# Stage of the maxima in a graph-attention layer: its window loop written out, with five product blocks in front and two and one by turns, and two groups of node values between the halves of a projection

## The reference

```python
xr = jnp.einsum('nd,rdf->rnf', x, W)
oi = xr[etype, dst]
oj = xr[etype, src]
qi = oi @ q
kj = oj @ k
alpha = jax.nn.leaky_relu(qi + kj, NEG_SLOPE)
m = jax.ops.segment_max(alpha, dst, num_segments=n_nodes)
e = jnp.exp(alpha - m[dst])
```

## Time and profile before

| | |
|---|---|
| median of 3 runs | 1886.23 us (1881.67 to 1899.82) |
| the profiled execution, its time | 1884.94 us |
| its span | 1883.2 us |
| TensorE matmul busy | 1677.3 us (89%) |
| VectorE busy | 1332.5 us (71%) |
| ScalarE busy | 775.4 us (41%) |
| GpSimd busy | 250.7 us (13%) |
| mean granted TensorE clock | 0.938 |

### The profile page before, as it was taken

One profiled execution on the slowest core, in us unless ns is written; L12 is line 12 of the kernel. 1 busy time (PEld: TensorE's weight loads), 2 busy tenths in 40 slices (PEclk: granted clock), 3 DMA queues, 4 the chain that ended last, 5 costly groups with the idle time before them and its releaser, 6 DMA issues.

```text
span 1883.2 us, 36980 instructions
## 1 busy us (share of the span) xinstructions
PE 1677.3 (89%) x10771; PEld 1230.7 (65%) x10772; DVE 1332.5 (71%) x2635; ACT 775.4 (41%) x1020; POOL 250.7 (13%) x268
## 2 busy tenths in 40 slices
PE   2799999999999999579999999877998889999976
PEld 1465677778755556369999999874554555555534
DVE  6777877758515899948888787861376267777776
ACT  2232112222105555258787777762121133333342
POOL 2200000000000111000000000001001023333334
PEclk9899999989998999789999999986999999999988
DMA  4111114233354343261004031123456350011112
GB/s 159 61 46 50 53 56 115 75 93 107 126 200 164 110 139 103 89 190 55 28 28 139 28 111 55 44 69 106 125 179 210 112 201 18 32 50 50 61 59 82
DMA packets 122819, 177.59 MB, mean 94 GB/s; under 512 B 12604, under 2 KB 96452, under 8 KB 122232
## 3 DMA queue, kind: packets, MB, share of 16 engines
q1 hardware_dynamic: 122744, 176.61, 29.0%
HBM read 118.75 MB, written 57.84 MB: 94 GB/s over the span
## 4 chain that ended last, share of the span: by engine, by line
PE 69%; DVE 12%; issue 9%; DMA 5%; ACT 2%; DVEq 2%; POOL 1%; SPq 1%; ACTq 0%; POOLq 0%
PE ps L1889 20%; PE ps L1947 7%; PE ps L1946 7%; PE ps L1670 6%; PE ps L1671 6%; PE ps L1672 6%; PE ps L1688 5%; PE ps L1752 3%; PE ps L1731 3%; DVE tt_junk L1417 2%; DMA xr_d<-ev 1%; PE ps L1809 1%; DVE oh_q L1282 1%; PE ps L1980 1%; DVE oh_p L1284 1%
## 5 line engine op out<-in xcount | busy, mean ns | idle before, releaser
L1889 PE MATMUL ps<-xrh,pf 128*128 (+1 forms) x2400 | 407.4, 334 | 30.9 <-DVE pf L1501 24.9
L1889 PEld LDWEIGHTS ps<-xrh,pf 128*128 128x128 f32 x2400 | 403.7, 195 | 34.7 <-issue 33.8
L1670 PE MATMUL ps<-w_hi,xt_hi 128*128 128x384 f16 x960 | 320.8, 334 | 31.2 <-DVE ev L1532 19.9
L1671 PE MATMUL ps<-w_lo,xt_hi 128*128 128x384 f16 x960 | 320.9, 334 | 0.0
L1672 PE MATMUL ps<-w_hi,xt_lo 128*128 128x384 f16 x960 | 320.4, 334 | 0.0
L1282 DVE TENSOR_SCALAR oh_q<-pat,codeT,neg_w 125x630 f16<-125x630 uint16 x420 | 200.0, 476 | 52.7 <-PE ps L1688 43.3
L1501 DVE SCALAR_TENSOR_TENSOR pf<-vb,CT 128x1260 f32<-128x1260 f32 x120 | 175.6, 1468 | 55.5 <-PE ps L1889 55.5
L1946 PE MATMUL ps<-x,ph 128*128 (+1 forms) x600 | 196.4, 327 | 19.4 <-POOL pl L871 19.4
L1947 PE MATMUL ps<-x,ph 128*128 (+1 forms) x600 | 197.9, 330 | 0.0
L1497 DVE SCALAR_TENSOR_TENSOR vb<-vb,tb 128x1260 f32<-128x1260 f32 x120 | 174.5, 1468 | 31.7 <-ACT vb L1064 30.6
L1417 DVE CUSTOM_DVE_ANT_0 tt_junk<-kbc,mb 126x1260 bf16<-126x1260 f32 x120 | 185.4, 1582 | 1.3
(11 more groups left out here) (226 smaller groups left out, 2323.1 us busy)
## 6 DMA issues: line engine op xcount, KB each, us to landing
qbc<-tq_d SPq DMA_DIRECT2D x12, 1260.0 KB, 5.8
wst<-in_L_gnn_W SPq DMA_DIRECT2D x12, 1152.0 KB, 7.4
xr_d<-ev SPq DMA_DIRECT2D x60, 192.0 KB, 2.0
xrh<-xr_d SPq DMA_DIRECT2D x4, 2880.0 KB, 15.9
x_d<-ev SPq DMA_DIRECT2D x60, 192.0 KB, 2.3
x<-x_d SPq DMA_DIRECT2D x3, 3840.0 KB, 13.6
mb_d<-mb SPq DMA_DIRECT2D x30, 310.1 KB
mb<-mb_d SPq DMA_DIRECT2D x30, 310.1 KB
```

The lines of the kernel that those rows point to most:

```text
L1670: pe.matmul(ps[:, bank, 0:CW], a_hi, hi[:, k, :], start=(k == 0), stop=False)
L1671: pe.matmul(ps[:, bank, 0:CW], a_hi, lo[:, k, :], start=False, stop=False)
L1889: mm = pe.matmul(out[b], pf[j][:, b * DB:b * DB + P], x, start=(first and b % 2 == 0), stop=False, skip_group_check=True)
```

## The change

The window loop is no longer a hardware loop on any engine but written out, and its order is new. Five blocks (`N0`) run ahead of window 0's; `products_of(w)` gives two blocks to even windows and one to odd ones, so that the 50 blocks of the loop are spread over all 30 windows. TensorE transposes the mask of window w + 2 (was w + 1) behind the blocks of window w. `maxima` writes straight to `mkt`, with four junk tiles in place of two, and waits for results further back. The node values of heads 3 and 2 are computed between the halves of the output projection. The high part of a weight chunk is made behind the last block of the chunk before it, and SyncE loads the next chunk behind the fifth store of each chunk. Cut to its core:

```diff
+        def products_of(w):
+            return range(N0 + (3 * w + 1) // 2, N0 + (3 * w + 4) // 2)
...
 # SyncE
-            loaded = 4
-            for m in range(2, loaded):
-                weights_load(sp, m)
...
+            weights_load(sp, 2)
+            def store_product(n):
+                sp.wait_ge(g_free, 6 * NB + n + 3)
+                store_xr(sp, n // NB, n % NB, n % 2)
+                if n in (N0 - 1, NB + N0 - 1, 2 * NB + N0 - 1):
+                    weights_load(sp, n // NB + 3)
+            store_mask(0)
+            for n in range(N0):
+                store_product(n)
+            for w in range(NW):
+                if w >= 1:
+                    store_mask(w)
+                for n in products_of(w):
+                    store_product(n)
...
 # ScalarE
-            w_hi_part(C_X + 1)
...
+            act.wait_ge(g_done, 6 * NB)
+            node_values(0)
+            node_values(1)
+            act.wait_ge(acc_out, 16 * 2 * NB)
             act.wait_ge(ct_in[0], 16 * 4)
...
+            def product_out(n):
+                xr_part(n, n // 2, n % 2)
+                if n % NB == NB - 1 and n // NB + 2 < 2 * R:
+                    w_hi_part(C_X + n // NB + 2)
+            def mask(w):
+                if w >= 2:
+                    act.wait_ge(mt_tr, w - 1)
...
+            def mask_out(w):
+                o = 1024 * (4 - 2 * (w % 2))
+                act.wait_ge(mt_tr, w + 1)
+                if w >= 2:
+                    act.wait_ge(mk_step, H * (w - 1))
+                    act.wait_ge(mb_out[w % 2], 16 * (w // 2))
...
+            mask(0)
+            node_values(2)
+            node_values(3)
+            mask_out(0)
+            mask(1)
+            w_hi_part(C_X + 1)
+            for n in range(N0):
+                product_out(n)
+            for w in range(NW):
+                if w >= 1:
+                    mask_out(w)
+                    if w == 20:
+                        act.wait_ge(ct_in[1], 16)
+                    if w + 1 < NW:
+                        mask(w + 1)
+                for n in products_of(w):
+                    product_out(n)
...
 # VectorE
+            for w in range(NW):
+                dve.wait_ge(mb_done, w + 1)
+                for h in range(H):
+                    q = H * w + h
+                    if h % 2 == 0:
+                        if w >= 1:
+                            dve.wait_ge(mk_step, q - 2)
+                        dve.memset(tick[:, h // 2:h // 2 + 1], 0.0)
+                    dve.tensor_tensor_reduce(out=tt_junk[h][0:WK, :], in0=kbc[0:WK, h, :], in1=mb[w % 2][0:WK, :], scale=1.0, scalar=2 * BIG,
+                                             op0=ALU.subtract, op1=ALU.max, accum_out=mkt[0:WK, h, w:w + 1]).then_inc(mk_step, 1)
...
 # TensorE
+                if c == 0:
+                    pe.wait_ge(kc_free, 1)
+                    pe.wait_ge(kr_out, NRG)
+                    pe.wait_ge(sel_done, 2)
+                    node_values(0)
+                    node_values(1)
...
+            def mask_rows(w):
                 pe.wait_ge(mt_done, w + 1)
+                if w >= 2:
+                    pe.wait_ge(mb_done, w - 1)
...
+            for n in range(2):
+                pe.wait_ge(kb_done, n + 1)
+                node_values(n + 2)
+            w1_product(0)
+            pe.wait_ge(kb_done, 3)
+            mask_rows(0)
+            for n in range(1, N0):
+                w1_product(n)
             pe.wait_ge(kb_done, H)
+            mask_rows(1)
+            for w in range(NW):
+                for n in products_of(w):
+                    w1_product(n)
+                if w + 2 < NW:
+                    mask_rows(w + 2)
```

More of the change, by code:

```diff
@@ L67 @@
 PW = 25
+N0 = 5
 TG = 7
@@ L173, in build @@
         kbc = place("kbc", [P, H, ND], F32, 91936)
-        tt_junk = [place(f"tt_junk{j}", [P, ND], BF16, 112096 + 2528 * j) for j in range(H // 2)]
-        mk4 = [place(f"mk4_{j}", [P, H], F32, 122208 + 32 * j) for j in range(2)]
+        tt_junk = [place(f"tt_junk{j}", [P, ND], BF16, 112096 + 2528 * j) for j in range(H)]
         e_int = place("e_int", [P, 3, 3, ET], I32, 98304)
@@ L193, in build @@
         patf = place("patf", [P, QN], F32, 122944)
-        qr = place("qr", [32, R * H, WD], F32, 119200)
+        qr = place("qr", [32, R * H, WD], F32, 122240)
         mr = place("mr", [32, H, WK], F32, 107328)
@@ L415, in build @@
         CH = chunks()
[L417 to L432, removed]
+        def products_of(w):
+            return range(N0 + (3 * w + 1) // 2, N0 + (3 * w + 4) // 2)
+        assert products_of(NW - 1)[-1] == 2 * PW - 1
         def window(eng, w):
@@ L628, in _, with store_mask @@
             load_windows(sp, 50, NWN, 1)
-            loaded = 4
-            for m in range(2, loaded):
-                weights_load(sp, m)
[L632 to L644, removed]
+            weights_load(sp, 2)
+            def store_mask(w):
+                sp.wait_ge(mb_done, w + 1)
+                sp.dma_start(mb_d[w, :, :], mb[w % 2][0:WK, :]).then_inc(mb_out[w % 2], 16)
+            def store_product(n):
[11 more added lines that the diff above has]
+                    store_product(n)
             def last_stores(v0, v1):
@@ L978, in _, with node_values @@
             act.sem_inc(ev_out[1], 16)
[L979 to L982, removed]
             w_hi_part(C_X)
-            w_hi_part(C_X + 1)
-            for n, h in enumerate(range(H - 1, -1, -1)):
+            def node_values(n):
+                h = H - 1 - n
+                b = 3 - 3 * (n % 2)
                 act.wait_ge(kb_mm, n + 1)
-                if n == 2:
-                    act.wait_ge(acc_out, 16 * 2 * NB)
-                act.activation(kbc[0:WK, h, :].rearrange("p (q n) -> p q n", q=3), ps[0:WK, 3 * (n % 2):3 * (n % 2) + 3, 0:ND // 3], ACT.Copy).then_inc(kb_done, 1)
+                act.activation(kbc[0:WK, h, :].rearrange("p (q n) -> p q n", q=3), ps[0:WK, b:b + 3, 0:ND // 3], ACT.Copy).then_inc(kb_done, 1)
+            act.wait_ge(g_done, 6 * NB)
+            node_values(0)
+            node_values(1)
+            act.wait_ge(acc_out, 16 * 2 * NB)
             act.wait_ge(ct_in[0], 16 * 4)
@@ L996, in xr_part @@
                 act.activation(ev[j][:, :], ps[:, 6 + j, 0:CW], ACT.Copy).then_inc(g_free, 1)
-            def mask(w, jw):
-                act.wait_ge(mt_tr, w + 1)
[L1001 to L1025, removed]
@@ L1817, in _, with node_values @@
             pe.wait_ge(ct_ev, NWN + 1)
+            def node_values(n):
+                h = H - 1 - n
+                for q in range(3):
+                    last = pe.matmul(ps[0:WK, 3 - 3 * (n % 2) + q, 0:ND // 3], sel[:, h, :, :, :].rearrange("p u r d -> p (u r d)"),
+                                     kq[:, q * ND // 3:(q + 1) * ND // 3], start=True, stop=True)
+                last.then_inc(kb_mm, 1)
             for c in range(2):
@@ L1832, in mask_rows @@
                 for a in range(NB):
                     n = min(P, ND - a * P)
-                    o = 1024 * (4 - 2 * jw) + a * P
-                    last = pe.transpose(psb[0:WK, o:o + n], mt[jw][0:n, a, :], identb[0:n, 0:n])
+                    o = 1024 * (4 - 2 * (w % 2)) + a * P
+                    last = pe.transpose(psb[0:WK, o:o + n], mt[w % 2][0:n, a, :], identb[0:n, 0:n])
                 last.then_inc(mt_tr, 1)
-            pe.wait_ge(kc_free, 1)
-            pe.wait_ge(kr_out, NRG)
@@ L1840, in _ @@
[L1840 to L1847, removed]
-            pe.wait_ge(kb_done, H)
@@ L1849, in _, with w1_product @@
[L1849 to L1861, removed]
-                        if after:
-                            mask_rows(w + 1, 1 - jw)
+            def w1_product(n):
+                if n % NB == 0:
+                    pe.wait_ge(w_lo_done, C_X + n // NB + 1)
+                pe.wait_ge(g_free, 6 * NB + n + 1)
+                product(C_X + n // NB, xt_hi, xt_lo, n % NB, 6 + n % 2).then_inc(g_done, 1)
```

34 lines of the change are left out of this document (9 added, 25 removed).

## The result

| | before | after |
|---|---|---|
| median | 1893.03 us (4 runs, 1881.67 to 1900.99) | 1989.79 us (4 runs, 1981.19 to 2005.10) |
| profiled execution, its span | 1884.94, 1883.2 us | 1990.22, 1988.5 us |
| mean granted TensorE clock | 0.938 | 0.928 |

The medians are of runs made side by side; of before these are the three shown with the prediction and one more. The changed kernel takes 1.052 times as long (95% interval 1.045 to 1.059), 96.8 us more by the medians.

What follows compares the result with a forecast made beforehand. It took TensorE, then VectorE, as the bound before, and TensorE and ScalarE waiting on each other after. 1884.94 us, plus 58 for later transposes of the maxima, plus 35 for clock falls, gave 1978 us; range 1925 to 2015.

Steps and rivals of the forecast that it cites:

- second half of the projection: Output projection, two groups of node values moved ahead of its second half: ends 5.9 us later (bounds 4.2 and 7.5).
- VectorE's first maximum: Start of the maxima, after window 0's mask row is copied out: at 582 us, against 583.3 before.
- rounds at full clock: Window loop, turns 1 to 28: 6.8 us with one block, 9.7 with two, 231 us in all.
- conversions of weights in the ring: Weight conversions on ScalarE behind blocks 9, 19 and 39 add 2.0 us each to the rounds: 6 us.
- the ring: Window loop: after each turn's last block TensorE waits 3.14 us while ScalarE evicts it, copies the mask row, makes the mask.
- the clock: Window loop: 28 stops of TensorE, 7/9 followed by a fall to half clock losing 1.6 us: 35 us (bounds 0, 56).
- from the end of block 48 to the transposes: End of the stage: blocks 49 to 53 follow without a wait, 5 x 2.92 = 14.6 us.
- the front: From the projection to the window rounds: VectorE starts at 582 us, blocks 5 and 6 run to 601.0 us.
- VectorE's part: Maxima: 5.6 to 5.8 us a window instead of 6.2 to 6.5, 18 us less work if VectorE is the bound.
- The rival in which VectorE sets the end: Window loop: masks are ready when TensorE asks, VectorE's pace puts the transposes at 774 us: 1864 us, 5%.
- the rival in which the clock holds: Window loop: TensorE's stops bring no clock fall: 1943 us, 1935 with node values at their cheap bound; 18%.
- The loops written out: Window loops: worth little, a loop turn costs VectorE some 0.26 us and TensorE nothing; starving by straight-line code set at nothing.

Runs made afterwards that it cites:

- e1: Changed kernel with ScalarE making the mask of window w + 2, not w + 1, in turn w, ahead of that turn's evictions: 1885.80 us, 0.9964 of before.
- e2: Changed kernel with TensorE transposing the mask of window w + 1, not w + 2, behind the blocks of window w: 1889.79 us, 0.9991 of before.
- e3: Changed kernel with 18 useless matmuls added on TensorE ahead of each turn's wait for the mask: 1953.15 us, 1.0307 of before.
- e4: Kernel before with only two of the four groups of node values moved between the halves of the output projection: 1895.72 us, 1.0011 of before.
- e5: Kernel before, window loops written out, with maxima straight into mkt, no copy and waits for older results: 1879.15 us, 0.9919 of before.
- e6: Kernel before with only its window loops written out on all four engines, same order: 1887.60 us, 0.9984 of before.
- e8: Changed kernel with mask w + 2 made in turn w, window 1's mask row earlier, all node values behind the projection: 1882.66 us, 0.9966 of before.
- e9: e8 with GpSimd's five weight subtractions in the stage of the maxima given to VectorE: 1876.04 us, 0.9886 of before.

## Why the prediction was right

It said 1978 us, 93 more than before; measured were 1989.79, and 96.8 more by the medians. Its steps, from T0 (534.5 in its own count):

| step | predicted | measured in after |
|---|---|---|
| second half of the projection | 5.9 us longer | 4.5 us |
| VectorE's first maximum | T0 + 47.5 | T0 + 49.5 |
| end of block 6 | T0 + 66.5 | T0 + 70.1 |
| TensorE's wait a turn | 3.14 us | 3.00 us |
| rounds at full clock | 6.8 and 9.7, 231 in all | 6.71 and 9.63, 228.8 |
| conversions of weights in the ring | 3 × 2.0 | 3 × 2.0 |
| the clock | 35 | 32.7 |
| from the end of block 48 to the transposes | 14.6 | 14.5 |
| transposes of the maxima | T0 + 353 | T0 + 352.0 |

That the two ends meet within 1 us is partly luck: the front came out 3.6 us longer than forecast, rounds, clock and the last five blocks together 4.6 us shorter.

**The ring** is what was forecast, and e1 and e2 show that it is the cause: with either end of it moved, all of the loss is gone. The 3.14 us were a sum of steps of the earlier trace rows; 3.00 is what the trace gives. The difference is in the step from the eviction to the mask row: 0.51 us in the row of before, where the mask row had to wait for transposes that ran from 588.40 to 589.13, and 0.38 in the ring (656.51 to 656.89), where they are long done. Timeline of TensorE in before:

```profile
588.40 0.73 PE L1835 MATMUL ps<-identb,mt 128*126 128x128 bf16 x10
```

**The clock** came to 32.7 us for 35, but by two errors that cancel. The rows of before gave seven falls in nine gaps, so 22 of 28 rounds at 1.6 us; in after 16 of 28 rounds are penalised, with 2.04 us on average and up to 2.95. Gaps of the very same 3.00 us are followed by a fall or not (666.12 full, 675.75 half), and what decides between them no run here shows; behind the three gaps of 5.01 us it fell each time. That the sum of the penalties is the clock's alone e3 does show.

**The front** was too short by 3.6 us at block 6. Half of that is a later start of block 2, T0 + 53.0 for the forecast T0 + 51.3. The other half is a fall of the clock that the sum had no term for: behind a gap of 2.02 us ahead of block 2 the clock is half from 597 to 600 us, and blocks 2 to 4 take 10.46 us (596.27 to 606.73) for 8.8. Timeline of TensorE in after, the first matmul of block 2:

```profile
596.27 0.34 PE L1662 MATMUL ps<-w_hi,xt_hi 128*128 128x384 f16 x1 [2.02 <-ACT ev L989]
```

VectorE's start was forecast 1.3 us earlier than before and came 0.7 later; e4 has the direction of it (the moved groups delay the first maximum by 4.0 us when nothing else is changed). Behind the moved groups themselves the clock fell in e4 and not in after.

**VectorE's part** was priced at 18 us of work and nothing on the time in the ring. The work is right (windows 5.58 us apart in e1, 0.6 less than before), the memset's 0.12 falls away too, and in after it shows only as idle time. Without the ring 7 to 13 us of it come through (e5 to e6, e5 to before).

**The rival in which VectorE sets the end** gave 1864 us, transposes at 774, so T0 + 239.5. e1 is that case, and has T0 + 254.2. The 14.7 us between are the later start (3.7) and the 12.3 us of idle time behind window 0, less 1.3. The prediction itself had named the idle time (mask_out(1) behind block 6) but left it out of this rival's price. In the rival in which the clock holds, the 1935 us for the cheap front do not follow: 4.2 us for 5.9 are 1.7 less, so 1941, and the lower end of the range, 10 below, would be 1931.

**The loops written out** were set at little, and e6 agrees: 0.9984, with 1 inside the interval. The rule on taken branches that stood beside it would win a fetch wait each turn; the 0.3 us a turn that VectorE's windows lose in e6 is all that shows of it.

The 8.7 us ahead of T0 and the 2.5 us behind the stage were in no term. The first varies by 24 us between profiled executions; where it comes from was not tried.

## What to carry to other kernels

When two in-order queues feed each other, write down for each hand-over how many turns ahead the one asks and how many turns ahead the other makes: if the consumer is moved one turn forward and the producer isn't, the engines take turns, whatever each gains by itself. Price such a stop twice, once for the idle time and once for what the clock takes afterwards; filling the gap with useless matmuls separates the two. Before reordering for an engine that is the bound, look at what holds single operations of it up: here five operations of GpSimd cost VectorE more than doing their work itself.

## What the runs showed of the hardware

- Behind 25 gaps of 3.00 us in TensorE's work, in the same pattern of rounds, the half clock came 13 times, and behind three gaps of 5.01 us each time, at a price of 1.3 to 2.95 us. With the gaps filled by matmuls, down to 0.08 us and to 2.09 at three, the clock read 1.00 from 623 to 860 us; in before it fell behind a gap of 1.98 us (927.00).
- Two groups of node values, together twelve float32 matmuls in the trace (24 rows, 420 columns), took 4.42 us at the same place in e4 and in after; the clock was half for 3.4 us behind them in e4 (0.50 from 539 to 542 us) and full in after.
- A subtraction of 128 × 2304 took GpSimd 4.55 to 5.07 us in e8 and VectorE 2.55 us in e9, and beside it on GpSimd a maximum of VectorE with two inputs in SBUF took up to 5.8 us in place of 1.46.
